# Value product's halves added by GpSimd in the last stage, and the value product issued behind the third scores in each step

## What is computed

```python
xn = _layernorm(x)
qu, ku, vu, qc, kc, vc = split(xn @ W_qkv.T)         # each: 8 heads x 512 tokens x 64
term1 = where(causal_mask, 0, (qc * SCALE) @ vu.T)
lookahead = where(causal_mask, sigmoid((qu * SCALE) @ ku.T), 0)
Su = term1 @ lookahead.T
scores = (qc * SCALE) @ kc.T - silu(Su)
attn = softmax(where(causal_mask, neg, scores))
out = (attn @ vc) joined over the heads @ W_out.T
h = silu(xn @ wg.T) * (xn @ wu.T)                    # 768 wide, integer weights / 127
result = x + out + h @ wd.T
```

## Time and profile before

| | before |
|---|---|
| median of 3 runs | 1165.88 us |
| profiled execution, device time | 1163.48 us |
| its span | 1161.8 us |
| TensorE matmuls busy | 1102.6 us (95%) |
| VectorE busy | 889.6 us (77%) |
| ScalarE busy | 771.6 us (66%) |
| GpSimd busy | 497.8 us (43%) |
| mean granted TensorE clock | 0.991 |

### The profile page before, as it was taken

The page is one execution under the profiler, slowest core; times in us unless marked ns, Lnnn a source line. Parts: engine busy times, 40 slices in busy tenths (PEclk is TensorE's granted clock), DMA queues, the critical chain, the costliest instruction groups (busy, mean ns, idle before and its releaser), DMA issues.

```text
span 1161.8 us, 21529 instructions
## 1 busy us (share of the span) xinstructions
PE 1102.6 (95%) x8000; PEld 995.2 (86%) x8000; DVE 889.6 (77%) x1855; ACT 771.6 (66%) x1387; POOL 497.8 (43%) x599
## 2 busy tenths in 40 slices
PE   5899999999999999999999999999999858999998
PEld 4788888888888888888888888888888757999997
DVE  5587787778777877778777777877787778778885
ACT  5577777777777777777777777777777845344443
POOL 0254555455555555555555555555555553000000
PEclk9999999999999999999999999999999979999999
DMA  7000100000000000000000000000000301333332
GB/s 244 1 10 7 32 10 10 11 27 10 11 15 23 10 10 21 18 10 10 28 10 10 10 28 11 10 11 28 10 11 10 128 19 50 121 121 120 99 111 73
DMA packets 30042, 43.88 MB, mean 38 GB/s; under 512 B 1520, under 2 KB 19184, under 8 KB 29936
## 3 DMA queue, kind: packets, MB, share of 16 engines
q1 hardware_dynamic: 29936, 42.47, 11.1%
HBM read 29.88 MB, written 15.47 MB: 39 GB/s over the span
## 4 chain that ended last, share of the span: by engine, by line
PE 86%; DVE 7%; ACT 4%; issue 1%; DMA 0%; POOL 0%; DVEq 0%; ACTq 0%; POOLq 0%
PE X L620 23%; PE X L544 20%; PE X L743 7%; PE X L658 7%; PE X L734 7%; PE X L629 6%; PE X L588 5%; PE X L604 4%; PE X L559 4%; DVE o_s L1182 4%; ACT o_low L922 3%; PE X L574 3%; PE X L535 1%; PE X L722 1%; DVE low_max L1105 0%
## 5 line engine op out<-in xcount | busy, mean ns | idle before, releaser
L620 PE MATMUL X<-L_s,T_s 128*128 128x128 f32 (+3 forms) x1920 | 278.2, 303 | 9.4 <-issue 9.4
L472 POOL TENSOR_SCALAR prob<-prob,inv 128x512 f32<-128x512 f32 (+3 forms) x256 | 278.3, 1104 | 17.4 <-DVE inv L1158 17.4
L620 PEld LDWEIGHTS X<-L_s,T_s 128*128 128x128 f32 x1920 | 266.3, 191 | 19.7 <-issue 9.6
L544 PE MATMUL X<-xT,W 128*128 128x512 f32 x960 | 236.7, 399 | 1.5 <-DVE xT L1194 1.4
L544 PEld LDWEIGHTS X<-xT,W 128*128 128x128 f32 x960 | 178.1, 191 | 41.3 <-DVE xT L1194 1.8
L892 ACT ACTIVATE gate<-X 128x1024 f32<-128x1024 f32 (+1 forms) x96 | 84.7, 883 | 129.6 <-PE X L620 129.6
L1132 DVE SCALAR_TENSOR_TENSOR gate<-gate,X 128x1024 f32<-128x1024 f32 (+1 forms) x96 | 99.5, 1037 | 73.3 <-ACT gate L892 73.3
L900 ACT ACTIVATE prob<-prob,least 128x512 f32<-128x512 f32 (+3 forms) x256 | 141.3, 563 | 8.5 <-DVE least L1146 8.5
L462 POOL TENSOR_SCALAR_AFFINE_SELECT T_s<-T_s 128x512 fp32r<-128x512 f32 x128 | 111.2, 890 | 78.9 <-DVE T_s L1125 78.9
L1125 DVE TENSOR_TENSOR T_s<-X,T_s 128x1024 fp32r<-128x1024 f32 (+1 forms) x96 | 97.5, 1043 | 49.0 <-ACT T_s L878 48.8
L454 POOL TENSOR_SCALAR_AFFINE_SELECT tanh_l<-tanh_l 128x256 f32<-128x256 f32 (+1 forms) x96 | 46.2, 497 | 205.7 <-ACT tanh_l L870 205.7
(11 more groups left out here) (81 smaller groups left out, 1894.4 us busy)
## 6 DMA issues: line engine op xcount, KB each, us to landing
xb<-in_L_attn_x SPq DMA_DIRECT2D x16, 512.0 KB, 4.0
heads_out<-o_s SPq DMA_DIRECT2D x32, 256.0 KB, 2.1
gate<-heads_out SPq DMA_DIRECT2D x8, 1024.0 KB, 5.4
tanh_l<-in_L_attn_x SPq DMA_DIRECT2D x8, 512.0 KB, 4.7
out<-prob SPq DMA_DIRECT2D x8, 512.0 KB, 3.2
W<-w_copy SPq DMA_DIRECT2D x3, 768.0 KB, 8.1
tanh_l<-in_L_attn_W_qkv SPq DMA_DIRECT2D x2, 512.0 KB, 5.2
gate<-in_L_attn_W_qkv SPq DMA_DIRECT2D x2, 512.0 KB, 7.3
```

The source lines that it names most:

```text
L472: last = pool.tensor_scalar(v, v, inv[:, h, w - 1:w], None, ALU.mult)
L544: last = pe.matmul(out, sh.W[:, a, k, cols], xT[:, c, k, :], start=(n == 0), stop=(n == 3 * KD - 1))
L620: last = pe.matmul(both[:, h, at:at + (J + 1) * P], T_s[:, h, a, to:to + P], L_s[:, h, c, WIDE[J + 1]:WIDE[J + 1] + (J + 1) * P], start=(J ...
```

## The change

In each step `attend` moves behind the third scores, next to the projections, and `TURNS` is made anew: the banks of L1 to Sc2 move up by one turn, and O takes banks 2 and 3 behind Sc0. The halves of O are no longer added on VectorE. ScalarE copies all 128 partitions of O (both halves) in one instruction to `o_s`, which now holds both; SyncE stores them with two DMAs to a `heads_out` of twice the size. In the second stage both halves are loaded, and GpSimd adds them, four instructions of 128x512 for each batch, ahead of its `take_rstd`. There are two sets of input buffers, so the load of the next batch starts one round sooner. In VectorE's step `low_L` 0 takes the place of `sum_o`, ahead of `minus_scores`. On ScalarE `high_T` 2 and the first exponentials move ahead of the copy, and the copy stands ahead of the projections.

```diff
-TURNS = [("L", 0, (0, 1)), ("T", 0, (2, 3)), ("T", 1, (4, 5)), ("O", 0, (6, 7)), ("L", 1, (0, 1)), ("L", 2, (2, 3)),
-         ("Sc", 0, (4, 5)), ("Sc", 1, (6, 7)), ("T", 2, (0, 1)), ("Sc", 2, (2, 3)), ("proj", QU, (4,)),
+TURNS = [("L", 0, (0, 1)), ("T", 0, (2, 3)), ("T", 1, (4, 5)), ("L", 1, (6, 7)), ("L", 2, (0, 1)), ("Sc", 0, (2, 3)),
+         ("Sc", 1, (4, 5)), ("T", 2, (6, 7)), ("Sc", 2, (0, 1)), ("O", 0, (2, 3)), ("proj", QU, (4,)),
...
# TensorE, step
                 term1(part, b, q, g, 1)
-                if back2:
-                    attend(part, b, q, g)
                 look_ahead(part, b, g, 1)
...
                     scores(part, b, q, g, 2)
+                if back2:
+                    attend(part, b, q, g)
# VectorE, step
                 low_T(g, 0)
                 low_T(g, 1)
-                if back2:
-                    sum_o(g - 2)
+                low_L(g, 0)
                 if back1:
                     minus_scores(g - 1, 0)
                     minus_scores(g - 1, 1)
-                low_L(g, 0)
                 low_T(g, 2)
# ScalarE, the copy
-            def copy_o_low(g, both=None):
+            def copy_o(g, both=None):
                 act.wait_ge(o_filled, 2 * g + 2)
-                if g > 0:
-                    act.wait_ge(o_copied, 2 * g)
+                if g >= 2:
+                    act.wait_ge(o_stored[g % 2], (g // 2) * 32)
...
-                act.activation(o_low[:, :, :], both[DH:P, :, :], ACT.Copy).then_inc(o_low_copied, 1)
+                act.activation(o_s[:, g % 2, :, :], both[:, :, :], ACT.Copy).then_inc(o_copied, 1)
# ScalarE, step
                 high_L(g, 0)
-                if back2:
-                    copy_o_low(g - 2)
                 tanh_of_L(g, 1)
                 tanh_of_L(g, 2)
                 high_L(g, 1)
+                high_T(g, 2)
+                if back1:
+                    exp_of(g - 1, 0)
+                if back2:
+                    copy_o(g - 2)
                 if part == LAST and q == 3:
                     high_weights(0)
                 if ahead:
                     high_proj(g + 1, QU, par)
-                high_T(g, 2)
-                if back1:
-                    exp_of(g - 1, 0)
                 if part == LAST and q == 3:
                     high_weights(1)
+                if back1:
+                    exp_of(g - 1, 1)
                 if ahead:
                     high_proj(g + 1, KU, par)
-                if back1:
-                    exp_of(g - 1, 1)
                 high_L(g, 2)
# SyncE
-                sp.dma_start(heads_out[bass.ds(g * P, P), :], o_s[:, par, :]).then_inc(o_stored[par], 16)
+                for half in range(2):
+                    to = heads_out[half, bass.ds(g * P, P), :].rearrange("(h d) t -> d h t", d=DH)
+                    sp.dma_start(to, o_s[half * DH:(half + 1) * DH, par, :, :]).then_inc(o_stored[par], 16)
...
-                sp.dma_start(o_in, rows(heads_out, b, INNER).rearrange("(n p) d -> p n d", p=P)).then_inc(o_loaded, 16)
+                for half, to in enumerate((o_in[b % 2], o_more[b % 2])):
+                    sp.dma_start(to, rows(heads_out[half], b, INNER).rearrange("(n p) d -> p n d", p=P)).then_inc(o_loaded[b % 2], 16)
...
                 if part != LAST:
-                    sp.wait_ge(o_split, OT * (b + 1))
+                    if part == FIRST:
+                        for stored in o_stored:
+                            sp.wait_ge(stored, 32 * BATCH * PAIRS // 2)
+                    else:
+                        sp.wait_ge(o_split, OT * b)
# GpSimd, second stage
             def ffn(b, part):
+                for m in range(OT):
+                    if m == 0:
+                        pool.wait_ge(o_loaded[b % 2], b // 2 * 32 + 32)
+                    pool.tensor_tensor(o_in[b % 2][:, m, :], o_in[b % 2][:, m, :], o_more[b % 2][:, m, :], ALU.add).then_inc(o_whole, 1)
                 if part != LAST:
                     ffn_ln.take_rstd(pool, b + 1)
# ScalarE, second stage
-                act.wait_ge(o_loaded, b * 16 + 16)
+                act.wait_ge(o_whole, b * OT + m + 1)
# VectorE: sum_o and its calls in ffn_first are gone
```

## The result

The changed kernel takes 1187.33 us (median of 4 runs, 1185.36 to 1189.63), against 1165.81 us before. The ratio is 1.0187, with a 95% interval of 1.0168 to 1.0207: 21.5 us slower, where 19.8 had been forecast. The profiled execution took 1187.24 us and spans 1185.1 us, 23.3 more than that of before.

What follows compares the result with a forecast made beforehand. TensorE's queue plus one stop at Sc1 was taken to bound a step; in the new order VectorE's queue would. 20.0 + 1.1 - 1.2 - 1.1 + 1.0 = +19.8 us, 1185.7 from the median; range 1176 to 1198.

Steps and rivals of the forecast that it cites:

- The walk through the step: Engine queues followed through a step's start in the new order: `attend` starts later, each step 0.69 us longer, 29 steps 20.0 us.
- three forecast waits: New TensorE stops per step: Sc0 and Sc1 for `low_T` (0.75 and 0.3 us), `attend` for `minus_scores` 0 (about 0.6).
- The removed wait: Sc1's stop for VectorE's sum of the value product's halves goes: -0.68 us a step.
- The two removed changes of rows: TensorE changes between products of 64 and 128 rows fall from four to two: -0.4 us a step.
- The last step: `low_L` 2, awaited by Su0, comes earlier, -1.2 us; `ffn_x(1)` no longer waits for the last `sum_o`, -1.1 us.
- The second round: Second stage: first `high_o` waits 0 to 2 us once for the doubled load and GpSimd's addition; +1.0 us taken.
- rival 3: GpSimd's additions hold up VectorE in the second stage: some 20 us on top of the forecast, 1206 us; chance 0.06.
- the shared port: VectorE and GpSimd in SBUF: VectorE loses at most 0.26 us, not blocked for a whole GpSimd instruction; at most 7.5 us more.
- Rival 1: TensorE's queue alone decides; each step gains the whole 1.08 us, 31 us in all, 1134 us; chance 0.12.
- Rival 2: Waits and gains cancel: `attend` starts near 431.2 instead of 431.9, time within 2 us of before; chance 0.04.

Runs made afterwards that it cites:

- e1: Changed kernel with VectorE's `low_L` 0 moved back behind `minus_scores` 0 and 1: 1168.32 us, steps of 28.82 us.
- e7: Changed kernel with one more VectorE instruction, like `low_L` 0 and writing an unread tile, between `low_T` 1 and `low_L` 0: 1253.47 us.
- e3: Kernel before with the new order alone; halves still added on VectorE, behind `minus_scores` 2, stored and loaded once: 1187.45 us.
- e2: Changed kernel with `attend`, `TURNS` and ScalarE's copy at their old places, additions still on GpSimd: 1151.87 us, steps of 28.19 us.
- e5: Kernel of e2 with Sc0 issued ahead of L2 instead of behind it, `TURNS` to match: 1143.32 us, steps of 27.93 us.
- e4: Kernel of e2 with Sc2 behind the projection QU, so two more changes of rows per step: 1175.35 us.
- e6: Kernel of e5 with ScalarE's `high_o` 0 and 1 and VectorE's `low_o` 0 later in second-stage rounds from the second on: 1142.77 us.

## Why the prediction was right, and where it wasn't

*The walk through the step held.* The changed step was forecast 0.69 us longer and is 0.73; the value product was to start at 7.76 us and starts at 7.74. Its chain (ScalarE's T0, VectorE's T0, T1, L0 and the scores, then O's banks) is the one that e1 and e7 move, in either direction, and e3 shows that nothing else of the change is needed for it. `low_T` 0 starts 2.98 us behind L0 (forecast: 3.0), and all three forecast waits are there, one of them only in the starts.

*The gains were real, and paid for more than once.* The removed wait was put at 0.68 us a step. e2, which keeps the additions on GpSimd and leaves the value product where it was, gains 0.48, since the wait for `minus_scores` 0 was next in line. e5, where Sc0's place takes that wait away too, gains 0.74. The two removed changes of rows are worth 0.4 us a step by the earlier trace rows and e4. What the new order costs is the 2.7 us of cover over ScalarE's and VectorE's work on L0, T0 and T1.

*Shown and only argued.* That `low_L` 0 in front of `minus_scores` costs 0.58 us of the 0.73 is shown by e1. That the other 0.15 is what the waits for `low_T` cost above the gains follows from e1's timeline, where no other wait is left; no kernel was run that takes it away and keeps the new order.

*The last step* was put at -1.2 and -1.1 us. Su0 starts 17.72 us into it instead of 19.08, -1.4, and the wait of the earlier trace rows at `ffn_x(1)` is gone, but from Su0 to `ffn_x(1)` only 0.75 us are gained: -2.1 together.

*The second round* was a term of the sum that was mis-sized: +1.0 was taken out of 0 to 2, and +2.0 measured. The wait that it named is there. `high_o` waits 1.99 and 0.63 us for GpSimd, whose first addition started when the second half had landed, 8 us behind its issue. But only 0.8 us of the round go with that wait. The other 1.2 are the `low_h` that an addition held up (e6), which the prediction had under rival 3 and not in this term.

*What I said of the shared port was wrong.* I bounded what GpSimd can do to VectorE at 0.26 us for an instruction, and said that the rows don't bear out a blocking by a whole GpSimd instruction. The 0.26 was the longest of a few cases and no bound: the 1477 ns of the earlier trace rows belong to an instruction that started 0.24 us into a mask of 0.64. In e7, where a mask of 1.02 us is met 0.44 us after its start, it is 0.44. In the second stage it is more. GpSimd's additions take 1.28 us where nothing holds them up, and 16 of the 48 `low_h` (L1220) meet one. Eight of them take 1.60 to 1.82 us, two 0.91 and 0.92, and six 0.68 to 0.69 as in the kernel before. The line over the whole run (durations in ns, least, median and longest):

```profile
L1220 DVE SCALAR_TENSOR_TENSOR L_s<-tanh_l,T_s x48: 676/686/1819, 987.5 to 1175.7; 128x512 fp32r<-128x512 f32 x48
```

One such pair in the timeline of the third round, VectorE and GpSimd:

```profile
1038.05 1.65 DVE L1220 SCALAR_TENSOR_TENSOR L_s<-tanh_l,T_s 128x512 fp32r<-128x512 f32 x1 [0.70 <-ACT T_s L968]
...
1034.40 6.45 POOL L507 TENSOR_TENSOR gate<-gate,T_s 128x512 f32<-128x512 f32 x4 [5.76 <-DMA T_s<-heads_out]
```

The third of these four additions starts at 1037.87, 0.18 us ahead of `low_h`, and ends at 1039.15, and `low_h` ends 0.55 us behind that. The rule of the Trainium skill ("SBUF — State Buffer", "SBUF: two separate sides") is that the instruction that starts first has the shared ports for all of its time and the other is blocked. For this pair the trace agrees with it. It isn't so for every GpSimd instruction that reads SBUF, and there the measurement decides: beside a scaling of the probabilities that runs already, VectorE isn't held up (numbers in the last section).

Rival 3 still fell, for another reason: it took each round's blocking as lost, half of it at least. The rounds behind the second take 23.3 us as before, since VectorE's delays there are in front of work that TensorE isn't waiting for. Its mechanism was there, and in the second round it cost 1.2 us; its price of some 20 us wasn't.

*Rival 1* (TensorE's queue alone) fell, as the value product does wait. Even e1, where it doesn't, takes 28.82 us a step and not the 1.08 us less than before that rival 1 gives, as the waits for `low_T` are left. *Rival 2* comes close to e1, which isn't the kernel that was forecast.

## What to carry to other kernels

Before a product is moved to save a wait or a change of array layout, ask what its time covers: here 2.7 us of matmuls hid the emptying of three PSUM tiles on two engines, and without them the queue of an engine that is busy only 71% sets the step. Walk the new order queue by queue from durations of the old trace, in particular with whatever is queued ahead of the instruction that frees the bank. A long wait removed shows the next one; e2 and e5 took two steps to get what one wait seemed to promise.

## What the runs showed of the hardware

- A VectorE instruction with two SBUF inputs that starts during a GpSimd instruction can be held up by it: 0.69 us became 1.65 beside an addition of two tiles, and 1.22 became 1.66 beside a mask with one input. Where VectorE starts first, GpSimd pays instead: the 1621 ns of a mask in the earlier trace rows, beside a median of 637, are of one that starts 0.11 us behind a `low_L`.
- Where the two start within 0.02 us, either can be the one that is held up: `low_h` took 1.82 us in the changed kernel and 0.68 in e5. One such meeting made a round 1.2 us longer.
- GpSimd's scaling by a column of factors (L472 in the kernel before, 1.56 us) doesn't hold VectorE up in this way: a `low_L` of 128x512 that starts 0.52 us into it takes 0.70 to 0.71 us, against 0.67 to 0.68 in the changed kernel, where the scaling starts behind it.
- In e7, a stop of 2.08 us before a product stands in all 30 steps, behind a shorter one of 0.60 us. In 8 of them TensorE's granted clock fell to the lower level behind it (0.59 over the product of the one shown), in the others it stayed (1.00). It cost 1.6 us each time. In steps 2 to 30 of the changed kernel, with two stops of 0.5 to 0.6 us each, it never fell.
- A change between products of 64 and of 128 rows costs TensorE some 0.2 us (e4's starts).
- The landing of a last store of 512 KB took either 3.5 or 4.8 us, and both values occur with the stores of before (3.5 before, 4.8 in e3) and with the doubled ones (3.5 in e1, 4.8 in e2).
